# Convolution kernel built in halves, four adapter buffers, and moved steps in a four-layer sequence kernel

## The chip, the core and the metric

One core of a Trainium2 chip runs the whole program in one launch. The metric is the device time in microseconds (us) of one execution. TensorE (PE) multiplies and also transposes, VectorE (DVE), ScalarE (ACT) and GpSimd (POOL) compute elementwise, and SyncE (SP) issues nearly all DMA transfers, in program order.

## What is computed

The reference passes x (64 sequences of 32 positions, 512 features) through four residual steps. Cut to what matters here:

```python
# layer 0: an S4D convolution over the feature axis (length 512, 32 channels = positions), then an fp8 linear
K = 2.0 * einsum('hn,hnl->hl', Cs, exp(P)).real      # 64 modes, kernel of 512 taps for each of 32 channels
y = irfft(rfft(u * mask) * rfft(K)) + u * mask * D
x = x + einsum('bsd,od->bso', y * mask, w_fp8 * scale)
# layer 1: an adapter matrix per sequence (ids 1 to 14 here), then a gated FFN with NF4-dequantised weights
w = weight[adapter_ids]; a = einsum('bij,bkj->bik', x, w)
x = x + einsum('bsh,dh->bsd', silu(a @ dq1.T) * (a @ dq2.T), dq3)
# layer 2: linear + top-2 LoRA experts, then a top-8 memory read with a gate from a variance (bn_stats) and a small MLP
# layer 3: per-feature gate from a masked mean and a 5-tap convolution, then linear + mixed low-rank experts
```

## The kernel before

Activations are held transposed, features on partitions, in X and Y (4 chunks of 128 features by 2048 tokens). The 2048 tokens go in four blocks (tb) of 512. All engines have their own instruction list; semaphores order them.

**Front.** DVE works out the modes, then the angle tables for all 32 channels at once: `trig` and `dec` (L1271 to L1276), a chain of small operations on 128x32 (up to about L1310), and the products with the coefficients (five operations, L1312 to L1317). ACT takes Exp and Sin of the tables. PE makes 512 taps of every channel in 32 small matmuls (semaphore p_k). DVE adds the skip term D (`d_k`, L1321), SP stores the taps to the DRAM buffer `kpad` in four transfers and reads them back as Toeplitz strips (L482), 16 strips (g) of two channels, five buffers. Ahead of these SP has issued the input in convolution order (`uc`, 4 MB), the first weights of layer 1, and all of X in one transfer of 4 MB (L466). The small transfer that clears the head of `kpad` stands behind it.

**Convolution and layer 0.** PE takes eight matmuls for each strip; six PSUM banks; DVE empties a bank with the mask (`conv_out`, L1387). Between d_k and the first `conv_out` DVE also computes the sort of the adapter ids, starts the first weight unit, and dequantises the fp8 weight w0 in five passes (L1394 to L1398). After strip 15 comes the fp8 linear: 16 products (tb, oc) of four 128x512 matmuls; DVE adds each to X (L1441).

**NF4 units.** All through layers 0 and 1, DVE and ACT together dequantise 15 units of weights, 15 levels each: ACT compares (L652, at most two levels ahead), DVE accumulates (L1374). Levels are dealt out by fixed numbers:

```python
NCV, NF0, NAD = 10, 26, 50      # levels in the convolution, in the fp8 linear, in the adapter stage
K_CONV = [min(max(g - 4, 0), NCV) for g in range(HG)]
K_FFN0 = [NCV + min(2 * (n + 1), NF0) for n in range(TB * DC)]
K_AD = [K_FFN0[-1] + (a + 1) * NAD // ADAPT for a in range(ADAPT)]
```

A unit starts (maximum per 64 weights, reciprocal, normalising; five DVE operations) five levels before the previous one ends. When a unit is complete PE transposes it (`turn_unit`, L861) and ACT copies it out (`evac_quant`, L660).

**Adapter stage.** Sequences are sorted by adapter and copied from X to Y: the first 4 by DVE, 4 by ACT (GX, GA), the others by POOL. PE works in 22 groups of up to 4 sequences, 16 matmuls of 128x128 each; ACT empties each group (L689) from four PSUM slots. Weights of an adapter (1 MB) lie in three buffers; two are loaded before the stage. SP loads the next when an adapter's last group is done, in one list with the loads of NF4 units and with the store of X (`keep`):

```python
if a >= NWS:
    done = sp.value_load(order[0:1, NB + a - 2:NB + a - 1], min_val=0, max_val=NGR)
    sp.wait_ge(s["p_ad"], done + 1)
```

**Layer 1** then is 44 up/gate products and 44 down products; in the last block of down products PE does `prepare` (small products of layer 2 and 3 weights). DVE adds the last block from PSUM to X (L1502) before layer 2 can begin.

**Layer 2** per tb: logits, linear, LoRA ranks, expert gates, `hgx`, a copy out by ACT (L761), query and MLP products, four transposes of 128 tokens (L1075) into two banks in turn for DVE's bn_stats (L1551), scores, MLP output. After the four blocks come `slices(0)` to `slices(3)`: layer-3 products of X with `wz`, four 128x512 matmuls each. **Layer 3** spreads a gate over partitions by `ones` times `gex` (`spread_gate`, four matmuls with 128 rows of which 64 are zeros), copied out by ACT (L808).

The trace records every fp32 matmul twice: 16 records are 8 matmuls.

## Time and profile before

| what | value |
|---|---|
| median of 3 runs (lowest, highest) | 952.16 us (951.54, 956.98) |
| the profiled execution's own time | 951.24 us |
| its span in the trace | 949.5 us |
| PE busy | 885.1 us (93%) |
| DVE busy | 579.8 us (61%) |
| ACT busy | 390.1 us (41%) |
| POOL busy | 86.9 us (9%) |
| mean granted clock of PE | 0.992 |

Read it so: the span is what the trace covers, from the first to the last instruction; the execution's own time is 1.7 us more. Busy shares are means over stages with different limits. The granted clock is a share of full speed (2.4 GHz).

### The profile page before, as it was taken

The numbers are of one execution on the slowest core, as the hardware profiler recorded it, in microseconds if no ns is written. First come the engines' busy times: TensorE is split into PE (matmuls) and PEld (weight loads), VectorE is DVE, ScalarE is ACT, GpSimd is POOL, SyncE is SP. The second block draws the span as 40 slices with busy tenths as digits, with TensorE's granted clock in tenths as the row PEclk, the third lists the DMA queues.
The fourth block names the chain that finished last, engine by engine and source line by source line (L and its number), as shares of the span: only waits on it lengthen the run. The fifth ranks groups of instructions, "written<-read, shape, count | busy, mean of one in ns | idle before, by whom it ended". The sixth has DMA issues, their size and how long they took to land.

```text
span 949.5 us, 10316 instructions
## 1 busy us (share of the span) xinstructions
PE 885.1 (93%) x3261; PEld 474.5 (50%) x3262; DVE 579.8 (61%) x880; ACT 390.1 (41%) x458; POOL 86.9 (9%) x127
## 2 busy tenths in 40 slices
PE   0299998999999999999999999999989999899998
PEld 0296448998444444444444444444434555354442
DVE  7889977886998888888997300000132354158444
ACT  2024637876777776676687100000012132241200
POOL 5100009600000000000000000002201011100000
PEclk9999998999999999999999999999999999999999
DMA  6873127562000000000000300024010000002022
GB/s 203 317 242 134 74 81 246 195 223 70 23 22 23 17 31 0 31 30 1 30 1 0 87 13 1 0 72 136 1 45 1 1 1 1 1 1 44 0 89 88
DMA packets 32967, 61.19 MB, mean 64 GB/s; under 512 B 5880, under 2 KB 8264, under 8 KB 31704
## 3 DMA queue, kind: packets, MB, share of 16 engines
q1 hardware_dynamic: 32216, 60.50, 18.8%
q0 software_dynamic: 704, 0.10, 0.3%
q8 instruction: 25, 0.41, 0.2%
q14 instruction: 22, 0.18, 0.1%
HBM read 51.07 MB, written 8.47 MB: 63 GB/s over the span
## 4 chain that ended last, share of the span: by engine, by line
PE 83%; DVE 12%; issue 2%; DMA 1%; ACT 1%; POOLq 1%; POOL 0%; SPq 0%; ACTq 0%; DVEq 0%
PE ps L820 81%; DVE acc L1374 2%; DVE T L1374 2%; PE ps L861 1%; DVE W2T L1218 1%; PE ps L1075 1%; DVE W2T L1224 1%; POOLq L603 1%; DVE W2T L1221 1%; DVE raw L1352 0%; DVE amax L1345 0%; DMA T<-kpad 0%; DVE W1T L1218 0%; DVE Up L1551 0%; DVE Yp L1659 0%
## 5 line engine op out<-in xcount | busy, mean ns | idle before, releaser
L652 ACT ACTIVATE above<-raw,cst 128x1024 bf16<-128x1024 f32 (+2 forms) x225 | 271.8, 1231 | 122.1 <-DVE acc L1374 46.5
L820 PE MATMUL ps<-Yp,W3T 128*128 (+2 forms) x872 | 183.9, 367 | 6.6 <-POOL Yp L605 2.6
L1374 DVE SCALAR_TENSOR_TENSOR acc<-above,acc 128x1024 f32<-128x1024 bf16 (+2 forms) x112 | 148.1, 1323 | 18.3 <-ACT above L652 11.6
L820 PE MATMUL ps<-Up,W1T 128*128 128x512 f32 x344 | 155.5, 594 | 3.0 <-DVE Up L1473 1.9
L820 PE MATMUL ps<-Up,W2T 128*128 128x512 f32 (+1 forms) x392 | 155.1, 593 | 0.0
L820 PEld LDWEIGHTS ps<-Yp,W3T 128*128 128x128 f32 (+1 forms) x872 | 121.9, 196 | 63.7 <-issue 61.5
L1374 DVE SCALAR_TENSOR_TENSOR T<-above,T 128x1024 f32<-128x1024 bf16 (+1 forms) x84 | 114.1, 1359 | 20.9 <-ACT above L652 18.0
L820 PE MATMUL ps<-X,W3T 128*128 128x512 f32 (+1 forms) x256 | 113.7, 602 | 0.6 <-DVE Yp L1659 0.6
L820 PEld LDWEIGHTS ps<-Up,W2T 128*128 128x128 f32 (+1 forms) x392 | 64.2, 177 | 83.0 <-issue 83.0
L820 PEld LDWEIGHTS ps<-Up,W1T 128*128 128x128 f32 x344 | 64.1, 190 | 82.5 <-issue 76.3
L1495 DVE TENSOR_TENSOR X<-X,Yp x16 | 4.6, 349 | 125.6 <-issue 125.6
L820 PEld LDWEIGHTS ps<-X,W3T 128*128 128x128 f32 (+1 forms) x256 | 48.8, 193 | 63.9 <-issue 62.0
L820 PE MATMUL ps<-Up,W3T 128*128 128x512 f32 (+3 forms) x240 | 63.9, 426 | 0.0
L614 POOL TENSOR_TENSOR X<-X,Yp x32 | 13.7, 459 | 477.3 <-issue 477.3
L820 PE MATMUL ps<-X,W2T 128*128 128x512 f32 x128 | 55.8, 594 | 0.0
L820 PEld LDWEIGHTS ps<-Up,W3T 128*128 128x128 f32 (+1 forms) x240 | 39.1, 191 | 23.6 <-issue 22.7
L699 ACT ACTIVATE Yp<-ps 128x2048 f32<-128x2048 f32 x3 | 5.6, 1877 | 109.0 <-PE ps L820 109.0
L710 ACT ACTIVATE Yp<-ps 128x512 f32<-128x512 f32 x40 | 23.5, 589 | 45.7 <-PE ps L820 45.7
L820 PEld LDWEIGHTS ps<-X,W2T 128*128 128x128 f32 x128 | 24.0, 190 | 29.0 <-issue 29.0
L820 PE MATMUL ps<-W1T,W2T 128*16 128x32 f32 x64 | 1.1, 241 | 33.8 <-DVE W2T L1317 33.8
L820 PE MATMUL ps<-Yp,raw 128*64 128x256 f32 (+2 forms) x128 | 29.1, 504 | 2.1 <-ACT Yp L761 2.0
L605 POOL COPY Yp<-X x44 | 28.9, 706 | 8.6 <-issue 8.6
(299 smaller groups left out, 753.4 us busy)
## 6 DMA issues: line engine op xcount, KB each, us to landing
W3T<-in_wa SPq DMA_DIRECT2D x11, 1024.0 KB, 6.3
raw<-in_w SPq DMA_DIRECT2D x20, 256.0 KB, 3.3
W3T<-kpad SPq DMA_DIRECT2D x9, 512.0 KB, 5.0
Up<-in_xconv SPq DMA_DIRECT2D x4, 1024.0 KB, 11.5
X<-in_xT SPq DMA_DIRECT2D x1, 4096.0 KB, 22.9
xkeep<-X SPq DMA_DIRECT2D x4, 1024.0 KB, 4.5
X<-xkeep SPq DMA_DIRECT2D x4, 1024.0 KB, 9.6
W3T<-in_wa SPq DMA_DIRECT2D x5, 768.0 KB, 4.6
```

Source lines behind the costliest of these rows:

```text
L603: bs = [pool.value_load(order[0:1, bass.ds(t * 4 + i, 1)], min_val=0, max_val=NB - 1) for i in range(4)]
L605: pool.tensor_copy(Y[:, :, bass.ds(t * (4 * S) + i * S, S)], X[:, :, bass.ds(b * S, S)]).then_inc(s["g_xs"], 1)
L614: pool.tensor_tensor(X[:, :, bass.ds(b * S, S)], X[:, :, bass.ds(b * S, S)], fo[tb][:, :, bass.ds(t * (4 * S) + i * S, S)], ALU.add).then_ ...
L652: nc.scalar.activation(above[0:h, m % 2, 0:w], raw[0:h, u % 2, 0:w], ACT.Relu, scale=STEEP, bias=cst[0:h, C_BND + i:C_BND + i + 1]).then_i ...
L710: nc.scalar.activation(sg[n % 2][0:h, :], ps[0:h, n % 2, :], ACT.Silu).then_inc(s["a_silu"], 1)
L820: return nc.tensor.matmul(o, l, r, start=start, stop=stop, **kw)
L861: last = nc.tensor.transpose(dst, src, ident[0:h, 0:h])
L1075: last = nc.tensor.transpose(ps[:, 3 - t % 2, c * P:(c + 1) * P], Y[:, c, tile(tb, t)], ident)
L1218: link(V.tensor_tensor(o, a, b, op))
L1221: link(V.tensor_scalar(o, a, x, y, op0, op1))
L1224: link(V.scalar_tensor_tensor(out=o, in0=a, scalar=x, in1=b, op0=op0, op1=op1))
L1374: V.scalar_tensor_tensor(out=ac, in0=src, scalar=float(STEPS[i]), in1=ac, op0=ALU.min, op1=ALU.add).then_inc(s["m_used"], 1)
```

## The change

What it does, part by part:

1. Angle tables, Sin, coefficient products, tap matmuls, skip term and stores are made in two halves of 16 channels each. The first half is stored before the second is finished; PE makes the second half (`make_k(1)`) before it starts on the strips, DVE adds its skip term after the start of unit 0, and SP stores it behind the fifth strip.
2. X is loaded in four pieces: two where all of it was, one behind strip 8, one behind strip 12. The dequantisation of w0 moves behind `conv_out(3)`, the load of unit 1 to strip 14. Levels: 4 in the convolution (10 before), 28 in the fp8 linear (26), 54 in the adapter stage (50).
3. Four adapter buffers in place of three, three of them loaded before the stage. X's last block is stored behind the load of adapter 4. DVE and ACT copy 3 sequences each (4 before). `turn_unit(1)` moves behind the last product of the fp8 linear, and ACT's copy of unit 1 behind its sequence copies.
4. The second half of `prepare` (`prepare_values`) moves behind the last down product; the waits for its results move behind the logits and ranks of block 0.
5. Layer 2: the four transposes use banks 3, 2, 5, 3, so that only the fourth waits for DVE; the MLP output waits for the third bn_stats. `slices(0)` is put in two parts into block 3, around the product with `hgx`.
6. Layer 3: two gates are held on the two partition halves and spread by a pair of matmuls of 64 rows each; the pair waits for two copies of ACT in place of one. A memset of POOL goes.

The diff, cut to its core:

```diff
-GX = 4
-GA = 4
+GX = 3
+GA = 3
...
-        NWS, WSINC = 3, [16, 32, 16]
-        WS = [[w3f[:, o + c * D:o + (c + 1) * D] for c in range(k)] for o, k in ((DC * D, DC), (2 * DC * D, DC - 1), (0, DC))]
-        WS[1].append(w1f[:, (NH - 3) * DC * P:(NH - 2) * DC * P])
+        NWS, WSINC = 4, [16, 16, 32, 16]
+        wd = w1f[:, (NH - 5) * DC * P:(NH - 1) * DC * P]
+        wb = w2f[:, (NH - 5) * DC * P:(NH - 4) * DC * P]
+        WS = [[wd[:, c * D:(c + 1) * D] for c in range(DC)], [w3f[:, DC * D + c * D:DC * D + (c + 1) * D] for c in range(DC)],
+              [w3f[:, 2 * DC * D + c * D:2 * DC * D + (c + 1) * D] for c in range(DC - 1)] + [wb],
+              [w3f[:, c * D:(c + 1) * D] for c in range(DC)]]
...
-        NCV, NF0, NAD = 10, 26, 50
+        NCV, NF0, NAD = 4, 28, 54
         UP_A, UP_B = 21, 21
         BANKS0 = [4, 5, 0, 1, 2, 3]
+        BANKS_ST = [3, 2, 5, 3]
...
+            def load_x(c):
+                sp.dma_start(X[:, c, :], A["xT"][c * P:(c + 1) * P, :]).then_inc(s["l_x"], 16)
+
             load_unit(0)
-            sp.dma_start(X[:, :, :], A["xT"].rearrange("(c p) n -> p c n", p=P)).then_inc(s["l_x"], 16)
+            load_x(0)
+            load_x(1)
...
-            sp.wait_ge(s["d_k"], 1)
-            for q in range(4):
-                sp.dma_start(kr[:, q * HQ:(q + 1) * HQ, :], ksb[q * 32:q * 32 + LA, :, :]).then_inc(s[f"l_kp{q}"], 16)
+            def store_k(f):
+                sp.wait_ge(s["d_k"], f + 1)
+                for q in range(4):
+                    h = f * HF + q * HE
+                    sp.dma_start(kr[:, h:h + HE, :], ksb[q * 32:q * 32 + LA, f * HE:(f + 1) * HE, :]).then_inc(s[f"l_k{'pq'[f]}{q}"], 16)
+
+            store_k(0)
...
                 if g == NS - 1:
+                    store_k(1)
+                if g == HG - 2:
                     sp.wait_ge(s["d_w0"], 1)
                     load_unit(1)
 
+                if g in (8, 12):
+                    load_x((8, 12).index(g) + 2)
...
-            load_adapter(0)
-            load_adapter(1)
+            sp.wait_ge(s["d_w0"], 1)
+            for a in range(NWS - 1):
+                load_adapter(a)
...
+            for a in range(NWS - 1, ADAPT):
+                if a == NWS - 1:
+                    for u in units_between(K_FFN0[(TB - 1) * DC - 1], K_FFN0[-1]):
+                        load_unit(u + 2)
                     sp.wait_ge(s["d_ord"], 1)
                     sp.wait_ge(s["p_ffn0"], TB * DC)
-                if a >= NWS:
-                    done = sp.value_load(order[0:1, NB + a - 2:NB + a - 1], min_val=0, max_val=NGR)
+                else:
+                    done = sp.value_load(order[0:1, NB + a - NWS + 1:NB + a - NWS + 2], min_val=0, max_val=NGR)
                     sp.wait_ge(s["p_ad"], done + 1)
                     sp.wait_ge(s[f"l_wa{a % NWS}"], WSINC[a % NWS] * (a // NWS))
                 load_adapter(a)
-                if a == 2:
+                if a == NWS:
                     keep(TB - 1)
-                    for u in units_between(K_FFN0[(TB - 1) * DC - 1], K_FFN0[-1]):
+                if a >= NWS:
+                    for u in units_between(K_AD[a - NWS - 1] if a > NWS else K_FFN0[-1], K_AD[a - NWS]):
...
-            act.wait_ge(s["d_ang"], 2)
-            nc.scalar.activation(trig, whole, ACT.Sin, scale=-turn1).then_inc(s["a_ang"], 1)
+            for f in range(2):
+                hs = slice(f * HF, (f + 1) * HF)
+                act.wait_ge(s["d_ang"], f + 2)
+                nc.scalar.activation(trig[:, hs, :], whole[:, hs, :], ACT.Sin, scale=-turn1).then_inc(s["a_ang"], 1)
...
+            pe.wait_ge(s["d_kz"], 2)
+            def make_k(f):
+
+                pe.wait_ge(s["d_pp"], f + 1)
+                for i in range(HE):
+                    for q in range(4):
+                        h = f * HF + q * HE + i
+                        last = mm(ps[q * 32:q * 32 + LA, 6 + f, i * LC:(i + 1) * LC], pc[:, h, :], trig[:, h, 0:LC], True, True)
+                last.then_inc(s["p_k"], 1)
+
+            make_k(0)
...
+            make_k(1)
             pe.wait_ge(s["l_u"], 16 * DC)
             for g in range(HG):
...
                 for u in turns_ffn0(n):
-                    turn_unit(u)
+                    if u == 0:
...
+            turn_unit(1)
             pe.wait_ge(s["ad_out"], NG)
...
+            prepare_values()
             pe.wait_ge(s["d_x2"], NB // 2)
             pe.wait_ge(s["g_x2"], NB // 2)
-            pe.wait_ge(s["a_kk"], 1)
-            pe.wait_ge(s["a_w16"], 1)
-            pe.wait_ge(s["a_v2"], 2)
...
+                    pe.wait_ge(s["a_ha"], TB)
+                    slices(0, range(0, 2))
...
+                    slices(0, range(2, DC))
...
-                    if tb or t >= 2:
-                        pe.wait_ge(s["d_st"], NT * tb + t - 1)
-                    else:
-                        pe.wait_ge(s["a_va"], 1)
+                    if t == 0:
+                        pe.wait_ge(s["d_st"], NT * tb) if tb else pe.wait_ge(s["a_va"], 1)
+                    if t == 3:
+                        pe.wait_ge(s["d_st"], NT * tb + 1)
                     if t == 1 and tb + 1 < TB:
                         pe.wait_ge(s["d_gl"], tb + 2)
                     for c in range(DC):
-                        last = nc.tensor.transpose(ps[:, 3 - t % 2, c * P:(c + 1) * P], Y[:, c, tile(tb, t)], ident)
+                        last = nc.tensor.transpose(ps[:, BANKS_ST[t], c * P:(c + 1) * P], Y[:, c, tile(tb, t)], ident)
...
+                pe.wait_ge(s["d_st"], NT * tb + 3)
...
-            def spread_gate(tb):
-                pe.wait_ge(s["d_gex"], tb + 1)
-                if tb >= 2:
-                    pe.wait_ge(s["a_g"], tb - 1)
+            def spread_gates(tb):
+                pe.wait_ge(s["d_gex"], tb + 2)
+                if tb:
+                    pe.wait_ge(s["a_g"], tb)
                 else:
-                    pe.wait_ge(s["a_zt"], tb + 1)
-                    pe.wait_ge(s["d_yd"], tb + 1)
-                mm(ps[:, tb % 2, :], ones[:, :], gex[tb], True, True).then_inc(s["p_gb"], 1)
+                    pe.wait_ge(s["a_zt"], 2)
+                    pe.wait_ge(s["d_yd"], 2)
+                for k, half in ((0, slice(YM, P)), (1, slice(0, YM))):
+                    mm(ps[:, k, :], ones[half, :], gex[tb + k], True, True).then_inc(s["p_gb"], 1)
...
+            def angles(f):
+
+                hs = slice(f * HF, (f + 1) * HF)
+                tt(trig[:, hs, 0:CMULT], f_[:, hs].unsqueeze(2).to_broadcast([P, HF, CMULT]), mul[:, hs, :], ALU.mult)
+
+            def whole_turns(f):
+
+                hs = slice(f * HF, (f + 1) * HF)
+                ts(trig[:, hs, CMULT:], trig[:, hs, LC:CMULT], 0.25, None, ALU.add, ALU.bypass)
+                ts(trig[0:MODES, hs, 0:LC], trig[0:MODES, hs, 0:LC], 0.25, None, ALU.add, ALU.bypass)
+                ts(whole[:, hs, :], trig[:, hs, :], ROUND, None, ALU.add, ALU.bypass)
+                V.scalar_tensor_tensor(out=whole[:, hs, :], in0=whole[:, hs, :], scalar=ROUND, in1=trig[:, hs, :],
+                                       op0=ALU.subtract, op1=ALU.subtract).then_inc(s["d_ang"], 1)
+
+            angles(0)
+            whole_turns(0)
...
+            def factors(f):
+
+                hs = slice(f * HF, (f + 1) * HF)
+                dve.wait_ge(s["a_ang"], 5 + f)
+                tt(trig[:, hs, 0:LC], trig[:, hs, 0:LC], dec[:, hs, 0:LC], ALU.mult)
+                tt(pc[:, hs, :], trig[:, hs, CMULT:], al[:, hs].unsqueeze(2).to_broadcast([P, HF, LA]), ALU.mult)
+                tt(pq[:, hs, :], trig[:, hs, LC:CMULT], be[:, hs].unsqueeze(2).to_broadcast([P, HF, LA]), ALU.mult)
+                tt(pc[:, hs, :], pc[:, hs, :], pq[:, hs, :], ALU.add)
+                V.tensor_tensor(pc[:, hs, :], pc[:, hs, :], dec[:, hs, LC:], ALU.mult).then_inc(s["d_pp"], 1)
+
+            def skip_term(f):
+
+                o = slice(f * HE, (f + 1) * HE)
+                dve.wait_ge(s["p_k"], f + 1)
+                dve.wait_ge(s["g_dsk"], 3)
+                V.tensor_tensor(ksb[:, o, :], ps[:, 6 + f, 0:HE * LC].rearrange("p (h c) -> p h c", c=LC), kdk[:, o, :], ALU.add
+                                ).then_inc(s["d_k"], 1)
+
+            factors(0)
+            angles(1)
+            skip_term(0)
+            whole_turns(1)
...
+            factors(1)
...
             start_unit(0)
-            dve.wait_ge(s["l_w0"], 32)
-            link(V.tensor_copy(h16a, w0u))
-            link(V.tensor_scalar(h16b, h16a, 0x7F, 7, ALU.bitwise_and, ALU.logical_shift_left))
-            link(V.tensor_scalar(h16a, h16a, 0x80, 8, ALU.bitwise_and, ALU.logical_shift_left))
-            link(V.tensor_tensor(h16a, h16a, h16b, ALU.bitwise_or))
-            V.tensor_scalar(w0, h16a.bitcast(f16), 256.0, None, ALU.mult).then_inc(s["d_w0"], 1)
...
+                if g == 3:
+                    dequantise_w0()
+                    dve.wait_ge(s["d_w0"], 1)
+            dve.wait_ge(s["l_x"], 16 * DC)
```

## Rows read from the trace of the kernel before

**Rows 1.** The waits of PE, whole span: waited for, us in total, times, longest.

```profile
PE ps L820 <- DVE W2T L1317: 33.8, 1, 33.8
...
PE ps L820 <- DVE X L1502: 3.5, 1, 3.5
```

**Rows 2.** The timeline of the first 43 us: start, us, engine, instruction.

```profile
13.62 1.75 DVE L1218 TENSOR_TENSOR W1T<-W2T,cst 128x1536 f32<-128x1536 f32 x1
...
17.85 2.29 DVE L1276 SCALAR_TENSOR_TENSOR W2T<-W2T,W1T 128x2048 f32<-128x2048 f32 x1
...
29.59 1.23 DVE L1218 TENSOR_TENSOR W1T<-W1T 128x1024 f32<-128x1024 f32 x1
...
34.90 0.42 DVE L1321 TENSOR_TENSOR W2T<-ps,W2T 128x256 f32<-128x256 f32 x1 [1.18 <-PE ps L820]
...
37.28 0.23 DVE L1333 TENSOR_SCALAR oneh<-cst,idc 64x17 f32<-64x17 f32 x1
...
42.24 6.87 PE L820 MATMUL ps<-Up,T 128*128 128x256 f32 x32 [4.16 <-DMA T<-kpad]
```

**Rows 3.** DMA issues of the page: count, KB each, median us to landing.

```profile
X<-in_xT SPq DMA_DIRECT2D x1, 4096.0 KB, 22.9
```

**Rows 4.** The timeline: first and last w0 pass, and the last mask copies.

```profile
39.37 1.23 DVE L1394 CAST acc<-W1T 128x2048 uint16<-128x2048 uint8 x1
...
44.92 1.23 DVE L1398 TENSOR_SCALAR W3T<-acc 128x2048 f32<-128x2048 f16 x1
...
82.43 1.91 DVE L1387 TENSOR_TENSOR Yp<-ps,mnat 128x512 f32<-128x512 f32 x2
```

**Rows 5.** Windows of three stages: us, busy and instructions by engine, clock, DMA.

```profile
42.20:82.50 40.30, 40.26 (x255) 38.39 (x256) 37.10 (x61) 12.54 (x12) 0.16 (x1) 1.00 0.60 203
84.40:141.40 57.00, 56.95 (x144) 25.89 (x144) 49.17 (x54) 29.51 (x28) 0.00 (x0) 1.00 0.31 110
141.40:231.40 90.00, 85.01 (x728) 84.58 (x728) 70.34 (x73) 65.85 (x77) 36.19 (x57) 0.96 0.55 194
```

**Rows 6.** The timeline around the first adapter groups.

```profile
143.81 0.91 PE L820 MATMUL ps<-Yp,W3T 128*128 x6 [2.46 <-POOL Yp L601]
...
144.91 0.39 SPq L502 DMA_DIRECT2D W3T<-in_wa  x1
...
155.51 4.67 PE L820 MATMUL ps<-Yp,W3T 128*128 x26 [2.55 <-POOL Yp L605]
```

**Rows 7.** Short windows behind idle times of PE; the granted clock is PEclk.

```profile
146.00:148.00 2.00, 2.00 (x12) 2.00 (x11) 1.91 (x2) 1.89 (x2) 2.00 (x2) 0.50 1.03 386
702.00:706.00 4.00, 4.00 (x6) 1.76 (x7) 0.88 (x5) 0.28 (x1) 0.00 (x0) 0.65 0.04 13
824.00:828.00 4.00, 2.03 (x7) 0.66 (x7) 0.00 (x0) 1.88 (x1) 0.24 (x1) 1.00 0.01 4
```

**Rows 8.** The waits of all engines from 142 to 232 us.

```profile
ACT Up L689 <- PE ps L820: 15.0, 8, 3.0
```

**Rows 9.** Groups by line and form, up to 240 us: busy us, mean ns.

```profile
L1374 DVE SCALAR_TENSOR_TENSOR acc<-above,acc 128x1024 f32<-128x1024 bf16 x42 | 51.3, 1220 | 9.1 <-ACT above L652 5.2 <-issue 2.7
```

**Rows 10.** The timeline in layers 2 and 3.

```profile
670.66 1.99 PE L820 MATMUL ps<-acc 32*128 32x512 f32 x10
...
737.12 1.25 PE L1075 MATMUL ps<-cst,Yp 128*128 128x128 f32 x8 [0.36 <-DVE Up L1551]
...
822.07 3.70 PE L820 MATMUL ps<-Up,raw 128*128 128x512 f32 x8 [0.94 <-DVE Up L1545]
...
827.73 5.58 PE L820 MATMUL ps<-Yp,raw 128*64 128x256 f32 x24 [1.97 <-ACT Yp L761]
...
879.06 3.81 PE L820 MATMUL ps<-W3T,ones 128*128 128x512 f32 x8
...
880.18 0.60 ACT L808 ACTIVATE Yp<-ps 128x512 f32<-128x512 f32 x1 [11.71 <-PE ps L820]
...
901.07 1.14 PE L820 MATMUL ps<-Yp,raw 32*128 32x512 f32 x8
```

More of the change, by code:

```diff
@@ L286, in build @@
         mx2, gm2 = w2f[:, 4928:4930], w2f[:, 4932:4934]
-        gex = [w3f[:, i * TW:(i + 1) * TW] for i in range(TB)]
+        gex = [w3f[(0 if i % 2 else YM):(YM if i % 2 else P), i // 2 * TW:(i // 2 + 1) * TW] for i in range(TB)]
         wT = w3f[0:E, 2048:3072]
@@ L596, in _ @@
             g0 = GX + GA
-            first = [pool.value_load(order[0:1, g0 + i:g0 + i + 1], min_val=0, max_val=NB - 1) for i in range(12)]
+            first = [pool.value_load(order[0:1, g0 + i:g0 + i + 1], min_val=0, max_val=NB - 1) for i in range(14)]
             pool.wait_ge(s["d_x1"], TB * DC)
@@ L1013, in turn_logits, with slices @@
                 nc.tensor.transpose(ps[:, 2, 0:P], lgT, ident).then_inc(s["p_lg"], 1)
+            def slices(tb, part=range(DC)):
+                if tb == 1:
+                    pe.wait_ge(s["a_q"], TB)
+                if tb == 2:
+                    pe.wait_ge(s["d_st"], TT)
+                pe.wait_ge(s["g_xc"], tb + 1)
+                for c in part:
+                    mm(ps[:, tb, :], wz[:, c, :], X[:, c, tok(tb)], c == 0, False)
             logits(0)
@@ L1086, in _ @@
                 last.then_inc(s["p_lr"], 1)
-            def slices(tb):
-                if tb == 0:
-                    pe.wait_ge(s["a_q"], TB)
-                if tb == 2:
-                    pe.wait_ge(s["d_st"], TT)
-                pe.wait_ge(s["g_xc"], tb + 1)
-                for c in range(DC):
-                    mm(ps[:, tb, :], wz[:, c, :], X[:, c, tok(tb)], c == 0, False)
             def slices_aux(tb):
@@ L1177, in _ @@
                 aux(n)
-            for tb in range(TB):
-                spread_gate(tb)
+            for tb in range(0, TB, 2):
+                spread_gates(tb)
             base(2)
@@ L1227, in _ @@
             V.memset(zpad, 0.0).then_inc(s["d_zp0"], 1)
-            V.memset(ps[:, 6, 0:HQ * LC], 0.0).then_inc(s["d_kz"], 1)
+            for f in range(2):
+                V.memset(ps[:, 6 + f, 0:HE * LC], 0.0).then_inc(s["d_kz"], 1)
             dve.wait_ge(s["l_s4"], 80)
```

89 lines of the change are left out of this document (38 added, 51 removed).

## The prediction

> **What bounds the kernel now.** I read the page first: PE is busy for 93% of the span, so time can come only from PE's idle time, from matmuls that run below their pace, or from matmuls taken out or put side by side. The waits of PE say where it is idle: 33.8 us of the first 42 us are one wait for DVE's tap factors, 3.5 us one wait for the last addition of layer 1 [rows 1]. The timeline of the first 43 us shows a single DVE chain and behind it, from the end of the skip term (34.90 + 0.42 = 35.32) to the first strip matmul at 42.24, 6.9 us of store and strip transfer [rows 2]. The windows by stage show the convolution with PE busy for 40.26 of 40.30 us and the fp8 linear for 56.95 of 57.00; the adapter stage has 85.01 of 90.00 and a mean clock of 0.96 [rows 5]. The timeline there gives two waits, 2.46 and 2.55 us [rows 6], and the short windows behind them a granted clock of 0.50 of full speed, 1.2 GHz; behind the 3.5 us at the start of layer 2 it is 0.65 over 4 us; an idle time of 1.97 us in layer 2 left it at 1.00 [rows 7, 10]. Everything between (layer 1) is PE-bound and not touched: its level counts are the same, since 4+28+54 is 10+26+50.
>
> **Part 1, halves.** A DVE operation of 256 columns takes 0.42 us, of 1024 columns 1.23, of 1536 columns 1.75 [rows 2]: some 0.15 us fixed, the rest by columns. The tables run from 13.62 to 17.85 + 2.29 = 20.14, 6.5 us. Half of that with its five fixed parts is 3.6, so 2.9 us earlier. The five products run from 29.59 to 33.72 (34.90 less the wait of 1.18): 4.1 us, half 2.4, so 1.7 earlier. They end at 29.1. The angles of the second half (0.95) fill DVE's wait for PE, and the first skip term ends near 30.4, 5.0 us earlier [rows 2]. Adding 6.9 us, strip 0 is there at 37.3. But now PE must do the second half of the taps first. DVE's whole list up to there ended at 37.51 [rows 2]; less the wait of 1.18, plus ten more fixed parts (1.5), gives 37.8; PE's 32 tap matmuls add some 0.7. The convolution starts near 38.6, gain 3.6 us: 5.0 at best, 2.4 if a split operation costs twice as much more. I take 3.5, since the list is counted and not guessed. Behind PE's new wait stands the whole convolution; behind SP's wait for the second skip term stand strips 5 to 15, and SP is free of it near 42, when strip 0 is just done and four others are in place; four more store issues cost nothing there. DVE's second skip term waits for PE's taps behind start_unit(0), which covers them.
>
> X: its 4 MB landed 22.9 us after an issue at 14.4, at 37.3 [rows 3], and the small clear of kpad behind it. Since 10.2 us some 8.8 MB had been asked for (uc, unit 0, w0, X), so about 325 GB/s: 2 MB less end 6.5 us earlier, near 31, before the taps are stored. With X in one piece the strips would stay held until about 37.5, so this edit is what lets the halves count. The other 2 MB come between strips: the DMA share in the convolution was 0.60 [rows 5], and 2 MB more is some 6.5 of 40 us, 0.76. I cost them at nothing; the cover is the lead of five strips, 12 us.
>
> **Part 2, DVE's list.** w0's five passes (39.37 to 46.15, 6.8 us) [rows 4] now stand behind mask copy 3. A strip takes PE 2.41 us (40.6 less 6.87 for the first two, by 14) [rows 2, 5]. Mask copy 3 can end near 51.6, w0 near 58.5, copy 4 near 59.5; PE needs that bank for strip 10 near 64.7. So no stall; cover gone it would cost 1:1. At the end of the stage two mask copies stood in line (1.91 us) [rows 4], now one: 0.5 us. In the fp8 linear PE has one unit less to transpose (0.9). DVE was busy for 49.17 us of 57.00 [rows 5], and two levels of 1.22 [rows 9] make 51.7; with the register reads ahead of the adapter stage between them it comes near PE's 56. I take off 0.4. Last addition to X: 3.5 + 0.5 + 0.9 - 0.4 = 4.5 us earlier.
>
> **Part 3, adapter stage.** The 90.00 us are 5.0 idle, 0.04 of 90 = 3.6 lost to the clock, and 81.4 of work [rows 5]. The second wait (2.55, at 155.51) is put down to POOL, whose copies for that group were long done; what ended last is the load of adapter 3, issued only at 144.91 in a burst of loads [rows 6]. With adapters 1 and 2 in place and 3 issued as soon as the linear ends, it has two groups (7 us) and the gather to land, so this wait goes, and the half-clock stretch behind it (1.8). The first wait keeps its gather, but transposes of unit 1 (0.9) stand in it and each of DVE and ACT copies one sequence fewer: some 1.4 us are left. The nearest row, 1.97 us idle, kept the clock [rows 7, 10]; I take 1.8 back. POOL starts two rows later in the order, and rows 7 and on are wanted only a group later. New stage: 81.4 + 1.4 + 0.9 = 83.7, gain 6.3. Against it: DVE has four levels more (5.0) and one unit start more (two passes of 1.23, three small ones: 3.2), 8.2 us, and the stage is 6.3 shorter. ACT's waits for PE, the room, were 15.0 us [rows 8]. 14.5 of 15.0 are used, and not all of it lies where it is wanted: ACT's last copies stand behind level 81, and up(0) behind them. I take 1.5 us for this (0 to 4). Gain 4.8.
>
> SP's adapter loads are queued behind two NF4 loads that wait for levels: before adapter 8's load it waits for level 44, which I put at 159 us (139, then 12 levels of 1.24, a unit start and the delays of four ACT copies), while adapter 4, after six groups, ends near 160.
>
> **Part 4.** The ten records of 32 rows (1.99) and one small product of 0.3 us, 2.3 in all, move into the wait of 3.5 [rows 1, 10]: gain 2.3, all covered; ACT has their copies done before the linear. The wait is then 1.2, and the clock may stay: (0.35 x 4 = 1.4 us in one window, some 1.7 in all) [rows 7]. Between 0 and 1.7 I take 0.8, since 32-row and 8-column matmuls are all that PE does around it.
>
> **Part 5.** In each block PE waited 0.36 us before transposes 3 and 4 [rows 10]. Those two took 1.25; now only the fourth stands behind the wait, so half of that, some 0.65 us; four blocks, 2.6. The MLP output's wait for the third bn_stats is 0.6 us before it is reached. Slices(0) is 8 records of 0.43, 3.4 us. Its first half (1.7) stands in a gap of 0.94 and delays hgx's product by 0.8, its second half stands in the gap of 1.97 [rows 10]: 3.4 - 0.8 = 2.6. PE then comes to the transposes of the probabilities 3.3 us sooner, about when DVE has them; 0.2 off. 2.4.
>
> **Part 6.** Four spreads take 3.81 us [rows 10]. Four 32-row matmuls of 512 columns (8 records) took 1.14 us, where one after another is 3.4 [rows 10]: row groups run side by side. Two pairs would take 2.0. But the second pair waits for two copies of ACT of 0.60 each, of which one alone was waited for: 0.95 + 0.2 + 1.2 + 0.1 + 0.95 = 3.4. Gain 0.4 (0 to 1.8). The Trainium skill (TensorEngine Tiling, Tiling Modes and PSUM Bottleneck) says both: two row tiles give up to 2x, but "Tiling speeds up TensorE but not PSUM evacuation"; by the first alone the gain would be 1.8, by the second the 0.4 of the rows.
>
> **The sum.** 4.5 + 4.8 + 2.3 + 0.8 + 2.6 + 2.4 + 0.4 = 17.8 us. From the profiled execution's own 951.24 that is 933.4; its own time is 0.9 below the median of the runs, 952.16, inside their spread. I say 933. A difference of 1% (9.5 us) is about what a measurement can tell.
>
> **Rivals.**
> 1. DVE and ACT bound the adapter stage. For it: room used 14.5 of 15.0. Against: four PSUM slots let ACT lag by three groups (10 us). If a third of the 15.0 lies where it can't be used, 5 us are lost instead of 1.5: 937. Chance 0.18.
> 2. The halves do not do what they are for: split operations cost more, or the strips are held by DMA, and the convolution starts near 41: 3 us of gain go, 936; with both this and rival 1, 940. Chance 0.12.
> 3. The clock falls in the shorter waits too, at the adapters, layer 2, and between the pairs of spreads: 1.8 + 0.8 + 1.7, 937. For it: waits of 1.97 and 2.46 us lie close together and had opposite results [rows 6, 7, 10]. Against: the new waits are near 1.3 us. Chance 0.1. The Trainium skill (TensorE: Matmul & The Clock Gate, What's actually happening) has the low clock as the default, which only activity releases; by it each shortened wait may still end in a slow stretch, which is this rival.
> 4. Slower than before: SP's one list. If level 44 or 59 comes late, adapter loads stand behind it. Adapter 8's load has some 9 us of room; if DVE lags by more, each of the seven loads left comes after PE wants it, and each costs a wait like 2.55 and a half-clock stretch of 1.8 [rows 5, 6]: 30 us, so 963. It decides from a lag of 9 us; I work out 1.5. Chance 0.03.
> The forecast itself, 929 to 936, has 0.57.
>
> **How the numbers follow.** Best ends: convolution 5.0, no lag, clock kept, spreads 1.8: 17.8 + 1.5 + 1.9 + 0.9 + 1.4 = 23.5, 928. Rivals 1 to 3 reach 940, two together 942. The range 927 to 942 leaves out rival 4 and the rarer sums. Faster by over 1% is below 942.6: 0.57 + 0.18 + 0.12 + 0.1 less the cases where two or three meet, 0.9; within 1%, 0.07; slower 0.03.
>
> **What would show it.** First strip matmul near 38.6; first product of the fp8 linear near 80.4; first adapter group near 139, no PE wait of over 1 us until the last, mean clock of the stage 0.99 to 1.00; first up product near 222 (231.5 before); the last window of layer 1 to 2 with one wait near 1.2 us; slices(0) inside block 3; spreads in two pairs with 1.3 us between. The prediction is wrong if PE waits for ACT's copies in the adapter stage, if the wait for the second taps is over 39.5, or if DVE ends the linear's additions 2 us behind PE.

## The result and the profile after

The changed kernel takes 941.26 us (median of 4 runs, 940.94 to 941.47), the kernel before 952.17 (4 runs, 951.54 to 956.98): ratio 0.9866, 95% interval 0.9839 to 0.9893. That is 10.9 us (1.1%) by the medians; 17.8 were forecast. The profiled execution took 940.94 us, its span is 939.2 (949.5 before), so 10.3 us are to be found in the trace.

The waits of PE, kernel after (waited for, us in total, times, longest), against [rows 1]:

```profile
PE ps L838 <- DVE W2T L1370: 31.4, 2, 29.5
PE ps L838 <- ACT Up L707: 6.0, 3, 2.8
...
PE ps L838 <- POOL Yp L618: 1.4, 1, 1.4
...
PE ps L838 <- DVE X L1573: 1.2, 1, 1.2
```

The wait for the last addition of layer 1 (now L1573) fell from 3.5 to 1.2, and the 2.55 us of [rows 6] are gone. The second line is new: 6.0 us for ACT's copies of adapter groups (L707), which PE never waited for before.

The front, in the timeline (start, us, engine, instruction), against [rows 2]:

```profile
29.47 0.63 PE L838 MATMUL ps<-W1T,W2T 128*16 128x32 f32 x32 [29.47 <-DVE W2T L1370]
...
30.54 1.73 SPq L484 DMA_DIRECT2D kpad<-W2T  x4
33.34 0.90 SPq L494 DMA_DIRECT2D T<-kpad  x2
37.83 0.63 PE L838 MATMUL ps<-W1T,W2T 128*16 128x32 f32 x32 [1.91 <-DVE W2T L1370]
38.38 3.88 PE L838 MATMUL ps<-Up,T 128*128 128x256 f32 x11
```

The first strip matmul runs at 38.38 (42.24 before), and what came last is DVE's second half of the factors, 37.8 as counted. The fp8 linear starts at 80.03 (84.40).

Windows (us, then busy us and instructions of PE, PE's weight load, DVE, ACT, POOL, then clock and DMA), against [rows 5]; the last row is from the first adapter group to the first up product:

```profile
38.30:79.00 40.70, 40.62 (x268) 38.50 (x256) 32.42 (x57) 6.79 (x6) 1.90 (x1) 1.00 0.73 248
80.00:137.00 57.00, 56.95 (x144) 26.00 (x144) 52.39 (x56) 30.72 (x28) 0.00 (x0) 1.00 0.37 130
...
138.37:226.98 88.61, 82.52 (x729) 81.62 (x729) 74.94 (x74) 69.99 (x78) 36.61 (x55) 1.00 0.54 183
```

The adapter stage took 87.67 us before, from 143.81 [rows 6] to the first up product at 231.48, and takes 88.61 now. Its clock rose from 0.96 to 1.00 and PE's busy time fell from 85.01 to 82.52; what was won there PE now waits for elsewhere. The timeline around the end of that stage:

```profile
219.45 0.91 PE L838 MATMUL ps<-Yp,W3T 128*128 x6 [1.32 <-ACT Up L707]
219.69 0.60 ACT L707 ACTIVATE Up<-ps  x1 [0.63 <-ACT Up L707]
220.19 2.18 ACT L670 ACTIVATE above<-raw,cst 128x1024 bf16<-128x1024 f32 x2
...
222.75 1.15 ACT L670 ACTIVATE above<-raw,cst 128x1024 bf16<-128x1024 f32 x1 [0.39 <-DVE T L1439]
...
223.88 0.60 ACT L707 ACTIVATE Up<-ps  x1
...
225.10 0.60 ACT L707 ACTIVATE Up<-ps  x1 [0.62 <-ACT Up L707]
...
226.32 0.60 ACT L707 ACTIVATE Up<-ps  x1 [0.62 <-ACT Up L707]
...
226.98 5.12 PE L838 MATMUL ps<-Up,W1T 128*128 128x512 f32 x8 [2.84 <-ACT Up L707]
```

PE was done with the groups near 223.1, with the transposes behind them at 224.1. ACT still had three group copies to make, standing in its list behind the level at 222.75; one after another they come 1.22 us apart: 0.60 of copy and 0.62 of the loop around it (for each group ACT reads a register and checks two semaphores). PE waits 2.84 us, and the eight records behind the wait take 5.12 us in place of 3.70.

The start of layer 2:

```profile
691.31 2.01 PE L838 MATMUL ps<-acc 32*128 32x512 f32 x10
693.25 0.43 PE L838 MATMUL ps<-above 48*64 48x128 f32 x2
694.85 1.89 PE L838 MATMUL ps<-X,l2r 128*8 128x128 f32 x32 [1.17 <-DVE X L1573]
696.67 5.79 PE L838 MATMUL ps<-X,raw 128*128 128x512 f32 x8
...
702.40 4.03 PE L838 MATMUL ps<-X,W2T 128*128 128x512 f32 x9
```

The two small groups (32 and 48 rows) lie where the wait was. But the logits took 1.89 where block 1's take 1.06, and the eight records behind them 5.79 where 3.60 to 3.70 is usual: about 2.9 us lost from 694.85 to 702.40 (7.55 us; 4.6 at full clock). The granted clock was 0.76, 0.50 and 0.89 in three windows of 4 us from 692 on.

Layer 2, block 3, and layer 3's gates, against [rows 10]:

```profile
816.29 3.60 PE L838 MATMUL ps<-Up,raw 128*128 128x512 f32 x8
...
821.85 5.58 PE L838 MATMUL ps<-Yp,raw 128*64 128x256 f32 x24 [0.25 <-ACT Yp L779]
827.27 2.05 PE L1121 MATMUL ps<-cst,Yp 128*128 128x128 f32 x16
...
869.24 1.13 PE L838 MATMUL ps<-W3T,ones 64*128 64x512 f32 x4
871.69 1.13 PE L838 MATMUL ps<-W3T,ones 64*128 64x512 f32 x4 [1.32 <-ACT Yp L826]
```

The four transposes are one run without a wait. Before the product with hgx (816.29) no wait is left of 0.94, and the wait of 1.97 before the next product is 0.25. The gates are two pairs with ACT's copies between.

Positions of the same product in both traces give the account (us earlier than before; the right column is the gain or loss since the row above):

| product | before | after | earlier | since |
|---|---|---|---|---|
| first strip | 42.24 | 38.38 | 3.9 | +3.9 |
| fp8 linear | 84.40 | 80.03 | 4.4 | +0.5 |
| first adapter group | 143.81 | 138.37 | 5.4 | +1.1 |
| first up product | 231.48 | 226.98 | 4.5 | -0.9 |
| first logits | 700.71 | 694.85 | 5.9 | +1.4 |
| linear of layer 2 | 706.99 | 702.40 | 4.6 | -1.3 |
| its last 1-column product | 837.36 | 830.88 | 6.5 | +1.9 |
| first transposes of probabilities | 852.21 | 842.30 | 9.9 | +3.4 |
| first gate | 879.06 | 869.24 | 9.8 | -0.1 |
| base products behind the gates | 882.72 | 872.75 | 10.0 | +0.2 |
| end of the span | 949.5 | 939.2 | 10.3 | +0.3 |

### The profile page after: what moved, and what is told of

The parts are those of the page before. It is cut to its first block, busy times and chain, and to the rows that moved or that the text cites. A ratio compares the mean times of both kernels' runs of the same rounds, so it can differ in the third digit from the quotient of the medians.

```text
span 939.2 us, 10335 instructions
## 1 busy us (share of the span) xinstructions
PE 882.4 (94%) x3261; PEld 472.0 (50%) x3262; DVE 581.7 (62%) x891; ACT 389.9 (42%) x458; POOL 85.0 (9%) x128
## 4 chain that ended last, share of the span: by engine, by line
PE 79%; DVE 15%; ACT 2%; issue 2%; ACTq 1%; DMA 0%; SPq 0%; DVEq 0%
PE ps L838 77%; DVE acc L1439 4%; DVE T L1439 3%; ACT above L670 1%; PE ps L883 1%; DVE W2T L1255 1%; PE ps L1121 1%; DVE raw L1416 1%; DVE amax L1409 1%; DVE W2T L1261 1%; DVE W2T L1258 1%; ACTq L704 0%; DVE acc L1445 0%; DVE Yp L1730 0%; DVE W2T L1322 0%
## 5 line engine op out<-in xcount | busy, mean ns | idle before, releaser
L838 PE MATMUL ps<-Yp,W3T 128*128 (+2 forms) x760 | 167.7, 376 | 5.7 <-ACT Up L707 3.1
L1439 DVE SCALAR_TENSOR_TENSOR acc<-above,acc 128x1024 f32<-128x1024 bf16 (+2 forms) x112 | 148.2, 1324 | 16.0 <-ACT above L670 12.2
L838 PEld LDWEIGHTS ps<-Yp,W3T 128*128 128x128 f32 (+1 forms) x760 | 106.1, 191 | 63.2 <-issue 61.9
L622 POOL COPY Yp<-X x44 | 31.1, 756 | 6.6 <-issue 6.6
```

The costliest lines, as they stand in the source:

```text
L622: pool.tensor_copy(Y[:, :, bass.ds(t * (4 * S) + i * S, S)], X[:, :, bass.ds(b * S, S)]).then_inc(s["g_xs"], 1)
L838: return nc.tensor.matmul(o, l, r, start=start, stop=stop, **kw)
L1439: V.scalar_tensor_tensor(out=ac, in0=src, scalar=float(STEPS[i]), in1=ac, op0=ALU.min, op1=ALU.add).then_inc(s["m_used"], 1)
```

## The experiments

Each kernel is the changed one with the edit shown, if nothing else is said. Ratios are to the kernel before, run beside it on the same chip. These chips ran the kernel before at medians of 952.4 to 953.7 us with a scatter of up to 8, so that under 3 us only positions in the traces tell. Each profile is of one execution; its own time is given where it lies far from the median.

**1. Four levels out of the adapter stage** (into the up products).

```diff
-        NCV, NF0, NAD = 4, 28, 54
+        NCV, NF0, NAD = 4, 28, 50
```

> The changed kernel with 50 levels in the adapter stage in place of 54 (4, 28, 50); the four levels go to the up/gate products. Theory A (the list of NF4 levels that DVE and ACT share, with ACT's group copies queued behind it, sets the adapter stage of the changed kernel): four levels of 1.24 us less ahead of the last group copies, so PE's waits for ACT (6.0 us) shrink by 4 to 5 us, first up product near 222.5 instead of 227.0, time near 937. Theory B (the adapter stage is held by weight loads or POOL's gather): no change, 941.

938.36 us (936.72 to 938.59), ratio 0.9847 [0.981, 0.9883]. The same end of the stage in its timeline:

```profile
220.27 1.04 PE L883 MATMUL ps<-cst,acc 128*128 128x128 f32 x8
221.41 3.70 PE L838 MATMUL ps<-Up,W1T 128*128 128x512 f32 x8
...
220.76 0.60 ACT L707 ACTIVATE Up<-ps  x1 [0.67 <-PE ps L838]
```

ACT's last copy waits for PE again, not PE for ACT; of PE's 6.0 us of waits for ACT one of 0.9 is left, earlier in the stage. The first up product runs at 221.41 in place of 226.98, 5.6 us earlier, with the first group at the same place (138.42), and at full pace. The stage takes 83.0 us, what the forecast had (from 139 to 222). So the four levels cost the changed kernel 5.6 us at this point. Not all of it stays: the levels are moved, not saved. At the first logits this kernel is 2.6 us ahead of the changed one (692.23 against 694.85), 1.7 of the rest being one slow stretch of the clock in layer 1; the medians of the times differ by 2.9.

**2. The four levels into the front instead.**

```diff
-        NCV, NF0, NAD = 4, 28, 54
+        NCV, NF0, NAD = 6, 30, 50
```

> The changed kernel with levels 6, 30, 50: four levels and one unit start (3.2 us) leave the adapter stage, two levels and the start go into the convolution, two levels into the fp8 linear. Theory A: 8.2 us less DVE work in the stage, which is then PE-bound (83.7 us from the end of the linear's last addition): first up product near 221.5, time near 936, if the convolution and the linear hide what they get; if they don't, the fp8 linear starts later than 80.0 and up to 3 us go there. Theory B: 941.

943.05 us (942.6 to 946.22; the profiled execution 946.22), ratio 0.9894 [0.9857, 0.9931]. Its PE waits:

```profile
PE ps L838 <- POOL Yp L618: 4.7, 1, 4.7
PE ps L838 <- DVE Yp L1452: 4.0, 1, 4.0
```

PE stands 4.0 us for the last mask copy (linear at 83.89), and 4.7 before the first group (147.23), for POOL's copies. These wait for DVE's additions to X, whose last two run, in DVE's timeline,

```profile
144.35 1.41 DVE L1512 SCALAR_TENSOR_TENSOR X<-ps,wsc,X 128x512 f32<-128x512 f32 x2
```

behind a unit start (139.87 to 143.05) that now falls into the linear; in the changed kernel the last one runs at 136.15 and waits for PE. DVE's list had hardly any room left in the front: 3.9 us later at the linear (the forecast had up to 3), 8.9 at the first group. The stage itself then takes 84.4.

**3. The kernel before with four adapter buffers alone.** Levels, counts of copied sequences, X and everything else as before; the loads of units around the adapter loads stand as in the change, and w0 is waited for before the first adapter load.

```diff
-        NWS, WSINC = 3, [16, 32, 16]
+        NWS, WSINC = 4, [16, 16, 32, 16]
...
-            load_adapter(0)
-            load_adapter(1)
+            sp.wait_ge(s["d_w0"], 1)
+            for a in range(NWS - 1):
+                load_adapter(a)
```

> The kernel before with the four adapter buffers alone (three loaded ahead of the stage, X's last block stored behind adapter 4), levels as before (10, 26, 50). Theory A: with no level added the buffers give what was forecast, the wait of 2.55 us and the half-clock stretch behind it: 4.3 us, time near 948. Theory B, if the second wait was POOL's gather and not the load of adapter 3: no gain, 952.

949.42 us (945.57 to 951.49, 10 runs; the profiled execution 951.49), ratio 0.9953 [0.9929, 0.9977]: 3.5 us less, where theory A had 4.3. From the first group (143.14) to the first up product (226.34) it takes 83.2 us, against 87.7: the buffers win 4.5 us, where the forecast had 2.55 + 1.8 = 4.35 for the second wait and the slow stretch behind it. Half-clock records still follow the first wait, of 2.5 us.

**4. The values' products back into the down products.**

```diff
                 if n == (TB - 1) * NH + 3:
                     prepare()
+                    prepare_values()
 
-            prepare_values()
             pe.wait_ge(s["d_x2"], NB // 2)
```

> The changed kernel with the second half of the preparations (prepare_values) back inside the last down products. PE's wait before layer 2 is then 3.5 us again and costs 2.3 us more. Theory C (the small matmuls in the wait, 32 rows high, double the half-clock stretch of layer 2 from 1.7 to 3.4 us lost): 1.7 us come back, so 0.6 us slower, near 941.9. Rival (the longer stretch has another cause): the full 2.3 us slower, near 943.6.

942.50 us (940.38 to 947.3; the profiled execution 947.3), ratio 0.9876 [0.9837, 0.9914]: a time between the two forecasts (941.9 and 943.6), and no difference to the changed kernel that the scatter lets through. In the timeline the wait is back:

```profile
701.62 1.90 PE L838 MATMUL ps<-X,l2r 128*8 128x128 f32 x32 [3.47 <-DVE X L1573]
703.45 5.51 PE L838 MATMUL ps<-X,raw 128*128 128x512 f32 x8
...
708.90 1.45 PE L838 MATMUL ps<-X,W2T 128*128 128x512 f32 x3
```

The wait is 2.3 us longer, the size of the products. The logits come 6.8 us later than in the changed kernel; by the windows of 4 us with a clock under 1.00 between 136 and 692 us (4 times the missing share, summed), 6.8 us went to the clock here and 1.7 there, which leaves 1.7, or 2.1 with the 0.46 us that the first up product was ahead. And with the values back the loss around the logits is there too: 7.3 us from 701.62 to 708.90, as it is in experiment 3 (7.2), where they were never moved. So the moved products are not needed for it.

**5. A full product in the wait before layer 2**, computed and not read.

```diff
             prepare_values()
+            pe.wait_ge(s["a_w16"], 1)
+            mm(ps[:, 6, :], ident, w3f[:, 0:512], True, True)
             pe.wait_ge(s["d_x2"], NB // 2)
```

The added wait for `a_w16` comes earlier than in the changed kernel, where it stands behind the ranks.

> The changed kernel with one more product: behind the small products of the values, in the wait for the last additions to X before layer 2, TensorE also does one full 128x128 by 512 product (two records, some 0.9 us) whose result nobody reads. In the changed kernel the clock was 0.51 and 0.64 of full speed over the 8 us around the first logits (3.4 us lost); in the kernel before it was 0.93 and 0.65 (1.7 lost). Theory A (small products of 32 rows leave the array idle enough to bring the clock down, and one full product in the wait of 1.2 us keeps it): linear start of layer 2 some 2.5 to 3.4 us earlier, 938 to 939. Theory B (the fall comes by chance or by the whole stretch of waiting, whatever one product does): no difference within 1 us, 941, with the slow stretch still there.

938.93 us (936.58 to 941.22), ratio 0.9859 [0.9829, 0.989]. In the timeline:

```profile
695.55 1.06 PE L838 MATMUL ps<-X,l2r 128*8 128x128 f32 x32
696.54 3.70 PE L838 MATMUL ps<-X,raw 128*128 128x512 f32 x8
```

Full pace, 4.64 us to the linear, which comes 2.2 us earlier than in the changed kernel. One profile; more below.

**6. Twelve levels out of the adapter stage** (4, 28, 42).

> The changed kernel with 42 levels in the adapter stage in place of 54 (4, 28, 42), the twelve others in the up products. With 50 the stage took 83.0 us (88.6 with 54). Theory A (at 50 levels the stage is already bound by TensorE, and four levels were exactly what was too much): the first up product comes at 221 to 221.5 as with 50 levels, no gain of its own, and the up products, which then have twelve levels more than in the changed kernel, make TensorE wait for DVE and ACT by several us more than the 1.9 seen with 50: total 939 to 944. Theory B (DVE still binds at 50, the levels cost 1.2 us each wherever they are): first up product near 216 to 218, total under 937.

940.89 us (938.37 to 943.88), ratio 0.9885 [0.9851, 0.9919]. First up product at 220.44, 1.0 earlier than with 50. Its waits of PE:

```profile
PE ps L838 <- DVE X L1537: 2.9, 4, 1.1
PE ps L838 <- DVE Yp L1537: 2.7, 3, 1.9
```

With 50 levels that was one wait of 1.9. From the first up product to the first logits it takes 475.2 us; with 50 levels it took 470.8, of which 1.7 went to one slow stretch of the clock (469.1 without it, in experiments 11 and 12). Eight levels less buy 1.0 us in one stage and cost 4.4 to 6.1 in the next: at 50 the adapter stage is already bound by PE, as theory A had it.

**7. Experiments 1 and 5 together.**

> 50 levels in the adapter stage and the full product in the wait before layer 2, together. With 50 levels alone the kernel took 938.4, and its profile showed no slow clock around the first logits. Theory A (the full product keeps the clock where it would fall): 936 to 938, at most the time of 50 levels alone and with less spread. Theory B (one product does nothing for the clock): 938.4 and up to 0.5 us more.

933.68 us (932.96 to 937.35), ratio 0.9806 [0.9777, 0.9836]; 4.64 us from logits to linear. The fastest kernel of the study, below both theories' bands.

**8. All of X ahead of the strips.**

```diff
-            load_x(0)
-            load_x(1)
+            for c in range(DC):
+                load_x(c)
...
-                if g in (8, 12):
-                    load_x((8, 12).index(g) + 2)
```

> The changed kernel with all four pieces of X issued where the change issues two (in place of two behind strips 8 and 12), so 4 MB ahead of the taps' store and of the first strips. Theory A (the transfers in front hold the head of the tap buffer, and so the strips, until X has landed near 37.5): first strip matmul at 41 to 42.5 against 38.4, some 3 us later, and all later positions with it: 944. Theory B (queues share, or the strips start in time anyway and TensorE waits for the second taps until 37.8): first strip matmul at most 1 us later, total 941 to 942.

944.94 us (944.44 to 946.19), ratio 0.992 [0.9889, 0.995]. The timeline:

```profile
30.50 1.73 SPq L484 DMA_DIRECT2D kpad<-W2T  x4
38.07 0.90 SPq L494 DMA_DIRECT2D T<-kpad  x2
...
42.07 4.18 PE L836 MATMUL ps<-Up,T 128*128 128x256 f32 x12 [3.67 <-DMA T<-kpad]
```

The taps are issued for storing at 30.50 as before the edit, but the strips only at 38.07 (33.34 in the changed kernel), and PE waits 3.67 us for them. Without the split of X nothing of the halves would be left: 42.07 against 42.24. Theory A.

**9. A second unused product, half an array wide, in layer 3** (on top of 7).

```diff
                 last.then_inc(s["p_wt"], 1)
+            mm(ps[64:128, 0, :], ident[:, 0:64], X[:, 0, 0:TW], True, True)
             for tb in range(TB):
                 ranks(tb)
```

> 50 levels and the full product before layer 2 (933.7), and a second unused product in layer 3: 128 rows by 64 by 512 columns, in the wait of 0.7 us behind the eight small transposes of the gate matrices and ahead of the 8-row rank products. There the clock fell to 0.5 to 0.88 over 6 us in the kernel without it (1.7 us lost). The product takes some 0.9 us, of which 0.2 is not covered. Theory A (small products bring the clock down, a large one keeps it): 1.7 - 0.2 = 1.5 us less, 932, and no slow stretch between 884 and 890. Theory B (half an array for 0.9 us is not enough, or the fall has another cause): 0.2 us more, 934.

936.67 us (935.62 to 938.39), ratio 0.9819 [0.9794, 0.9845]. The timeline there:

```profile
887.94 1.14 PE L838 MATMUL ps<-Yp,raw 32*128 32x512 f32 x8
889.64 8.83 PE L838 MATMUL ps<-X,W3T 128*128 128x512 f32 x16 [0.56 <-DVE Yp L1733]
```

The 32-row products keep full pace (1.14, in 7 they took 2.09), but the 16 records behind take 8.83 where 16 take 7.1 elsewhere. Counted from the eight small transposes ahead, the slow stretch came 2 us later than in 7, and it cost the same 1.7 us. The time is 3 us above that of 7, where theory B had 0.2; the trace has 1.2 of it ahead of the first logits (693.43 against 692.24). And the product of 5 did not prevent everything here: 5.47 us from logits to linear. Theory A fell for this place.

**10, 11. The changed kernel, and experiment 1's kernel, profiled once more.**

> The changed kernel itself, unaltered, profiled once more. Theory A (the slow clock around the first logits belongs to its order of work): from the first logits to the linear of layer 2 again 7 to 7.6 us, as in the first profile, where the full clock gives 4.6. Theory B (it comes and goes between executions): any value from 4.6 to 7.6.

> The changed kernel with 50 levels in the adapter stage, unaltered, profiled once more. Theory A (it keeps the clock around the first logits because it comes there otherwise, or always): 4.6 us from the first logits to the linear of layer 2, as in its first profile. Theory B (it was chance): 6 to 7.6 us. The first up product at 221.4 again in both.

The changed kernel: 940.71 us, 7.56 us from logits to linear, as the first time. The one with 50 levels: 936.2 us, 6.24 us, where its first profile had 4.63; first up product at 221.12. So the loss at this place differs between executions of one kernel (theory B), at least with 50 levels.

**12. Experiment 1's kernel in five rounds.**

> 50 levels in the adapter stage without the unused product, timed in five rounds, to set beside the same kernel with the product (ratio 0.9806 to the kernel before). Theory A (the product keeps the clock in most executions, worth 1 to 3 us): ratio 0.983 to 0.985. Theory B (the product does nothing): ratio 0.979 to 0.982, that is 933 to 935 us. Its first timing gave 0.9847, so A's band is where it was; a value between is no answer.

938.4 us (932.92 to 938.55), ratio 0.9826 [0.9798, 0.9855]: between the bands, no answer. Its profile has 6.12 us from logits to linear.

All profiles with the changed order there, without the unused product: 7.55, 7.56, 7.40, 6.07, 6.24, 6.12, 4.63, 4.63, mean 6.28; with it 4.64, 4.64, 5.47, mean 4.92. The product looks worth 1.4 us, but three profiles and overlapping intervals (0.9806 with, 0.9847 and 0.9826 without) don't show it. Nor is the difference between 933.7 and 938.4 all at this place: in layer 3 near 890 us, far from the product, experiment 7's profile lost 1.7 us to the clock and the three of experiment 1's kernel 3.4 each (windows of 4 us, summed as in experiment 4).

## Why the prediction was right in kind and high in size

It said 933 with a range of 927 to 942; the time is 941.26. That lies 0.7 us inside the slow end of the range and outside 929 to 936, which the prediction held likeliest; the prediction reached that end by two rivals together, and two did happen, rival 1 above its price and rival 3 in part. The 0.7 us is less than the 0.9 us by which the front and part 5 came out better than forecast, so that the range holds the time is partly luck. The sign that the prediction itself gave for being wrong came true: PE waits for ACT's copies in the adapter stage (6.0 us, 3 waits). By its steps:

- **Part 1, halves: right.** First strip 3.9 us earlier (forecast 3.5), and for the reason given: PE waits for the second factors until 37.8. That X would hold the strips until about 37.5 is shown by experiment 8 (issued at 38.07).
- **Part 2, DVE's list: right.** Tail of the convolution 0.5 (0.5), from the linear to the first group 1.1 (0.8, from the forecast's 80.4 and 139). The 4.0 and 4.7 us of experiment 2 show that little cover was left beyond that.
- **Part 3, adapter stage: the step that failed.** "I take 1.5 us for this (0 to 4)", for DVE's and ACT's longer lists. Of the gain of 4.8, 0.3 was to show ahead of the first group (139) and 4.5 behind it (222.2); measured behind it is -0.9: 5.4 us short, most of what is missing. What the stage was to win is there: the second wait is gone, the clock is 1.00, and experiment 3 shows 4.5 us for the buffers alone (4.35). The lag is not 1.5 but 1.5 + 5.4 = 6.9 us, and experiment 1 takes 5.6 of it away. That is above the term's upper end of 4 and above rival 1's 5. The error was to spend ACT's 15.0 us of waits for PE [rows 8] as if either engine could fill them. DVE and ACT work on the levels in turns, and each waits for the other. The waits from 137 to 232 us in the changed kernel:

```profile
ACT above L670 <- DVE acc L1439: 7.6, 9, 3.3
...
DVE T L1439 <- ACT above L670: 6.0, 6, 1.6
DVE acc L1439 <- ACT above L670: 5.1, 5, 2.6
ACT Up L707 <- ACT Up L707: 4.4, 7, 0.6
```

Inside the stage DVE is busy for 74.94 us and waits 10.8 for ACT: 86 of 88.6. "DVE has 8.2 us more" came out as 6.8 (74.94 less 68.16). Where ACT's 15.0 us went can be added up, stage against stage: its waits for PE fell to 0.6; it was busy for 5.6 more (69.99 less 64.40), waited for DVE for 5.7 more (12.1, 6.4 before), and stood 3.8 more in the loop between two copies that come one after another (4.4, seven times; 0.6 before). The forecast counted work alone. The longest of ACT's waits for DVE, 3.3 us, is a unit start of DVE (it stands ten levels ahead of the end of the unit before, not five); before, none was over 0.7:

```profile
143.70 1.22 DVE L1409 TENSOR_REDUCE amax<-raw 128x16 f32<-128x1024 f32 x1
...
148.24 1.15 ACT L670 ACTIVATE above<-raw,cst 128x1024 bf16<-128x1024 f32 x1 [3.33 <-DVE acc L1439]
```

Experiment 1 shows that the four levels are the cause of the 5.6 us. How they cost it, hand-over and loop beside DVE's own 4 x 1.22 = 4.9 us of work, is read from these waits, and no run takes the three apart. Rival 1 was therefore the case that happened, priced too low.
- **Part 4, values: right as a move, too sure in the clock.** The wait fell by 2.3 (3.5 to 1.2). The 0.8 us that the clock should give back did not come: from the logits to the linear full pace is 4.63 us, the kernel before lost 1.65 there, the changed kernel 2.9 in both its profiles. That is rival 3 at this place. But the loss differs from execution to execution. With the old order it was 1.65, 2.6 and 2.65 (the kernel before, experiments 3 and 4), with the new order anything from none to 2.9, mean 1.65 of eight profiles (6.28 less 4.63). So how far this part missed is in part chance; the error of the forecast was to read the size, up to 1.7, from one profile.
- **The first up product** lost another 1.4 us to the clock (5.12 against 3.70), a consequence of part 3 that stood in no term. With it the clock's account is even: up to PE's last product, in windows of 4 us summed as in experiment 4, it cost 6.8 us before and 6.8 after, where the forecast had counted 4.4 as won back (1.8 twice in the adapter stage, 0.8 in layer 2).
- **Part 5: right.** The table's 1.9 over the four blocks is 4 x 0.6 for the transposes (2.4; forecast 2.6) less 0.5 for the slices inside block 3. Behind it the slices give 3.4, so 2.9 in all (forecast 2.4).
- **Part 6: right, in size nothing.** 0.2 us (0.4). The second pair waits 1.32 us for ACT; the matmuls side by side are not the limit. Two row groups did run side by side: a pair, four records, took 1.13 us, where half of the eight records of before is 1.9. The Trainium skill (TensorEngine Tiling, Theoretical Speedup and PSUM Bottleneck), cited in the prediction for both, has up to 2x for two row tiles, and no faster copies out of PSUM; the trace agrees with both, and the second decides.
- **Rival 4** did not occur: PE waited for no adapter load. Rival 3's own sum (1.8 + 0.8 + 1.7 on top of 933.4) is 937.7, not 937.

By the profiles 17.8 - 10.3 = 7.5 us are missing: 5.4 in the adapter stage, 0.9 between the first up product and the logits (2.3 forecast, 1.4 found, the slow stretch behind the new wait), 2.1 in the clock at layer 2 (0.8 not gained, 1.3 lost); better by 0.6 up to the first group and by 0.3 in part 5; what is left nets to nothing. The forecast's sum with the stage as measured would have been 933.4 + 5.4 = 938.8.

## What to carry to other kernels

Idle time of an engine in a stage is room for more work only if that work does not pass between two engines: where two engines hand pieces to each other, their waits for each other, and the gaps of their loops, take part of the room. How much was not forecast by any rule tried here: DVE's busy time plus its waits for ACT, 82.5 us in the kernel before, plus the 8.2 of the forecast gives 90.7, and 88.6 was measured; from experiment 3's 78.0 the same sum gives 86.2. And with the same 50 levels ACT waited 12.2 us for DVE in experiment 1 and 6.8 in experiment 2. So try one or two counts of pieces. Four of them moved over a stage boundary made the stage 5.6 us shorter here, more than the buffers did (4.5), though the next stage gave part of it back. Splitting a chain of computation into halves wins only what the transfers issued ahead of it let through, so split those too (3.7 us here).

## What the runs showed of the hardware

**The same wait has two outcomes for the clock.** In layer 1 PE waits 1.93 us once, at the same product in every kernel. The eight records behind it, in two of the 14 profiles (experiments 3 and 6):

```profile
471.66 5.40 PE L824 MATMUL ps<-Up,W1T 128*128 128x512 f32 x8 [1.93 <-DVE Up L1477]
```

```profile
473.88 3.70 PE L838 MATMUL ps<-Up,W1T 128*128 128x512 f32 x8 [1.93 <-DVE Up L1544]
```

In 6 of 14 the stretch fell to 1.2 GHz for a while and cost 1.7 us, in 8 not. The wait of 1.97 us in layer 2, which the forecast took as one that keeps the clock, stands in two profiles: the 24 records behind it took 5.58 us in the kernel before and 7.22 in experiment 3. Waits of 1.3 us between full products (the first group, the gates) never did in the changed kernel's family; the wait of 2.8 us before the first up product did in all five profiles that have it. The Trainium skill (TensorE: Matmul & The Clock Gate, What's actually happening) calls the count of slow matmuls at a kernel's start run-variable; here the same shows in the middle of a kernel. So a wait near 2 us should be priced with a chance, some 0.4 x 1.7 us, and not by the one profile at hand, as [rows 7] was read for the forecast.

**Small products can have a slow stretch behind them with no wait at all.** In experiment 3's profile PE works without a wait on products of 48, 32 and 8 columns or rows between 664.8 and 669.5 us; in the next windows, full products again:

```profile
668.00:670.00 2.00, 2.00 (x12) 1.34 (x11) 0.76 (x2) 0.75 (x2) 1.37 (x4) 1.00 0.00 0
670.00:672.00 2.00, 2.00 (x4) 0.87 (x3) 0.77 (x3) 0.57 (x3) 0.42 (x1) 0.55 0.00 0
672.00:674.00 2.00, 2.00 (x4) 0.79 (x3) 0.00 (x0) 0.00 (x0) 1.68 (x4) 0.60 0.00 0
```

Experiment 4, with the same products in the same place, shows it too (0.62 in one window of 4 us, 1.7 us lost), the kernel before does not. In layer 3, around products of 8 and 32 rows and a wait of 0.7 us, a slow stretch stands in all 14 profiles, the kernel before included, and costs 1.7 us in ten of them and 3.4 in four. In experiment 7's the products themselves show it, 2.09 us in place of 1.14:

```profile
885.70 2.09 PE L838 MATMUL ps<-Yp,raw 32*128 32x512 f32 x8
```

A busy PE in the trace is thus no proof that the clock stays. What exactly decides was not settled; experiment 9 only moved such a stretch.
